# Moving the slice-weight products behind the row tiles of a graph-attention block loop on one Trainium2 core

## The reference, cut to what matters

```
x = x + gnn(layernorm(x), edges)
x = x + ffn(layernorm(x))

gnn:  support = x @ W;  r = sigmoid(support @ a2);  gated = r * support
      out  = segment_sum(edge_weight * gated[dst], src) / segment_sum(edge_weight * r[dst], src)
      l    = softplus(out @ a1);  out = elu(max(out, 0) + l * min(out, 0))

ffn:  w     = softmax((x @ W_x + b_x) @ W_slice ...) over 64 slices, for each of 8 heads
      token = sum over all nodes of w * (x @ W_fx), divided by the sum of w
      attention among the 64 tokens of a head, then out = w @ tokens @ W_out + b_out
```

## Time and profile before

| what | value |
|---|---|
| device time, median of 3 runs | 1400.97 us (1393.98 to 1402.22) |
| profiled execution: span from the first to the last instruction | 1658.8 us |
| PE busy | 1228.8 us, 74% of the span |
| DVE busy | 1036.5 us, 62% |
| POOL busy | 898.6 us, 54% |
| ACT busy | 540.6 us, 33% |
| mean granted TensorE clock | 0.851 |

### The profile page before, as it was taken

How to read it: one execution, slowest core, us unless ns; L and a number is a source line. 1 busy time by engine, 2 the same in 40 slices (tenths; PEclk the granted TensorE clock), 3 DMA queues, 4 the chain that set the end, 5 groups by cost and what they waited for, 6 DMA issues and landing times.

```text
span 1658.8 us, 22400 instructions
## 1 busy us (share of the span) xinstructions
PE 1228.8 (74%) x6239; PEld 983.0 (59%) x6239; DVE 1036.5 (62%) x2696; ACT 540.6 (33%) x1992; POOL 898.6 (54%) x895
## 2 busy tenths in 40 slices
PE   3797565767667668778688778786688676777998
PEld 2686464656666667756355555554456454555787
DVE  8778585766776766563466666565666656666422
ACT  2354243442442432401133323332333322333232
POOL 0476755555565455575666666666666666663000
PEclk9799778888889788877798989887888788888999
DMA  7123333634344344453534334533343433332122
GB/s 236 43 70 54 92 98 108 106 107 118 98 119 110 91 115 109 112 115 89 107 106 106 106 101 114 101 107 104 104 112 99 104 99 108 102 101 59 37 76 72
DMA packets 163423, 166.44 MB, mean 100 GB/s; under 512 B 84678, under 2 KB 135898, under 8 KB 163309
## 3 DMA queue, kind: packets, MB, share of 16 engines
q0 software_dynamic: 39712, 108.02, 24.9%
q1 hardware_dynamic: 102428, 37.71, 9.6%
q10 hardware_dynamic: 21168, 19.35, 3.9%
HBM read 136.86 MB, written 28.14 MB: 99 GB/s over the span
## 4 chain that ended last, share of the span: by engine, by line
issue 41%; PE 22%; DVE 14%; another core or an unknown queue 14%; ACT 5%; DMA 1%; POOL 1%; SPq 1%; POOLq 0%; DVEq 0%; ACTq 0%
PE bank L1733 22%; DVE S L1302 2%; DVE neg L1340 1%; ACT big L1675 1%; DVE ag L1313 1%; DVE lg L1328 1%; DVE hm L1323 1%; POOL rows L844 1%; ACT S L1656 1%; DMA rows<-gated_rows_dram,ring_i 1%; ACT xT L1662 1%; SPq L626 1%; ACT pos L1634 1%; DVE neg L1345 0%
## 5 line engine op out<-in xcount | busy, mean ns | idle before, releaser
L844 POOL DMA_INDIRECT rows<-gated_rows_dram,ring_i x516 | 512.4, 993 | 282.4 <-issue 144.7
L1733 PE MATMUL bank<-rows,S 128*128 128x257 f32 (+1 forms) x2254 | 580.2, 398 | 47.4 <-issue 21.6
L1733 PEld LDWEIGHTS bank<-rows,S 128*128 128x128 f32 x2254 | 439.6, 202 | 157.7 <-issue 75.0
L751 POOL DMA_INDIRECT rows<-gated_rows_dram,lg x294 | 287.5, 978 | 240.3 <-PE bank L1733 114.5
L1733 PE MATMUL bank<-big 128*104 128x128 f32 (+3 forms) x1824 | 250.7, 305 | 85.2 <-ACT big L1516 44.3
L1733 PEld LDWEIGHTS bank<-big 128*104 128x104 f32 (+2 forms) x1824 | 246.2, 210 | 92.2 <-issue 89.5
L1733 PE MATMUL bank<-Wxs,xT 128*128 128x512 f32 x196 | 148.0, 898 | 103.8 <-ACT xT L1662 103.8
L1516 ACT ACTIVATE big<-big 128x52 f32<-128x52 bf16 x768 | 180.0, 325 | 13.6 <-ACT ovr L1571 12.2
L1302 DVE TENSOR_SCALAR S<-iota,lof,srec 128x128 f32<-128x128 f32 x588 | 165.2, 357 | 3.2 <-remote 3.1
L1733 PEld LDWEIGHTS bank<-Wxs,xT 128*128 128x128 f32 x196 | 47.3, 266 | 158.2 <-ACT xT L1662 112.7
L1313 DVE TENSOR_TENSOR ag<-bank,ovr 128x257 f32<-128x257 f32 x49 | 20.9, 427 | 191.6 <-PE bank L1733 97.5
(11 more groups left out here) (261 smaller groups left out, 1486.9 us busy)
## 6 DMA issues: line engine op xcount, KB each, us to landing
overflow_sums_dram<-ovr ACTq DMA_DIRECT2D x98, 128.5 KB
rows<-gated_rows_dram,ring_i POOLq DMA_INDIRECT x516
gated_rows_dram<-rows SPq DMA_DIRECT2D x49, 128.5 KB, 2.5
ovr<-overflow_sums_dram SPq DMA_DIRECT2D x49, 128.5 KB
rows<-gated_rows_dram SPq DMA_DIRECT2D x49, 128.5 KB
out_dram<-S SPq DMA_DIRECT2D x48, 128.0 KB, 1.7
rows<-gated_rows_dram,lg POOLq DMA_INDIRECT x294
res<-in_x_dram SPq DMA_DIRECT2D x1, 4352.0 KB
```

Of the source, the lines that this page charges most:

```text
L751: pool.indirect_dma_start(rows[:, turn(n), :], None, gtab[:, :], bass.IndirectOffsetOnAxis(ap=ring1[:, n:n + 1], axis=0)).then_inc(s_row[t ...
L844: pool.indirect_dma_start(rows[:, slot(b, u), :], None, gtab[:, :], bass.IndirectOffsetOnAxis(ap=ring_i[:, b // CH % 2, n:n + 1], axis=0)) ...
L1733: return nc.tensor.matmul(o, l, r, start=start, stop=stop, skip_group_check=True)
```

## The change

Four edits:

- In the PE loop `logits(b-1)` moves from between tiles 6 and 7 to between tiles 10 and 11, in front of the block's last row tile; `own` stays behind tile 7.
- `scored` uses the mark of tile 11 in place of that of tile 7.
- In ACT's `main`, `crossed(b-1)` moves from in front of `expo` to behind the normalisation (`xn`), in front of `keep`.
- `xn` has four buffers (`XB`) in place of three. To make room, `ring_r` and `lof` (edge places, read as per-partition scalars) lie in the columns of `Ws2`, a weight tile that only stage 1 uses.

```diff
+XB = 4
...
-        ring_r = sb("ring_r", [P, 2, U])
+        ring_r = Ws2[:, 96:96 + 2 * U].rearrange("p (k t) -> p k t", k=2)
...
-        lof = sb("lof", [P, 2, CH * TQ])
+        lof = Ws2[:, 0:2 * CH * TQ].rearrange("p (k t) -> p k t", k=2)
...
-        xn = sb("xn", [P, 3, F])
+        xn = sb("xn", [P, XB, F])
...
         def scored(b):
-            return after(b, 2, MARKS[1], s_lm)
+            return after(b, 2, MARKS[3], s_lm)
...
                 if b < LAST:
                     own(b + 1)
-                if b:
-                    crossed(b - 1)
                 if b >= 2:
                     expo(b - 2)
...
                 act.wait_ge(s_rs, b + 1)
-                if b >= 3:
-                    act.wait_ge(*summed(b - 3))
-                a.activation(xn[:, b % 3, :], res[:, b, :], ACT.Identity,
+                if b >= XB:
+                    act.wait_ge(*summed(b - XB))
+                a.activation(xn[:, b % XB, :], res[:, b, :], ACT.Identity,
                              bias=col(NM), scale=col(RS)).then_inc(s_xn, 1)
+                if b:
+                    crossed(b - 1)
                 if b >= 3:
                     keep(b - 3)
...
                     cross(b - 1)
-                segment(b + 1, 3, 7)
+                segment(b + 1, 3, 8)
+                own(b + 1)
+                segment(b + 1, 8, TQ - 1)
                 if b:
                     logits(b - 1)
-                segment(b + 1, 7, 8)
-                own(b + 1)
-                segment(b + 1, 8, TQ)
+                segment(b + 1, TQ - 1, TQ)
```

More of the change, by code:

```diff
@@ L1952, in cross @@
                 for c in range(2):
-                    t = nc.tensor.transpose(bank[6][:, c * P:(c + 1) * P], xn[:, b % 3, c * P:(c + 1) * P], ident[:, :])
+                    t = nc.tensor.transpose(bank[6][:, c * P:(c + 1) * P], xn[:, b % XB, c * P:(c + 1) * P], ident[:, :])
                 if b + 2 > LAST:
@@ L1979, in sums @@
                 for c in range(lo, hi):
-                    m = mm(bank[2 + c // 2][:, (c % 2) * F:(c % 2 + 1) * F], w[:, c * P:(c + 1) * P], xn[:, b % 3, :], False, False)
+                    m = mm(bank[2 + c // 2][:, (c % 2) * F:(c % 2 + 1) * F], w[:, c * P:(c + 1) * P], xn[:, b % XB, :], False, False)
                 if hi == NP2 and b + 4 > LAST:
```

## The result

| kernel | median, us | runs | lowest to highest |
|---|---|---|---|
| before | 1399.16 | 20 | 1393.96 to 1405.24 |
| after | 1404.74 | 20 | 1397.74 to 1413.88 |

The ratio is 1.0036, with a 95% interval of 1.0021 to 1.0051: 3 to 7 us slower, 5.6 by the medians. The forecast was 1406 us (+5), "same" by the 1% bound. The median, the sign and the size agree with it. Whether they do so for the reasons given is what the rest of this text asks.

A forecast was written before the change was run, and what follows sets the result against it. The prediction took POOL's indirect gathers, 1.258 us from start to start, to bound the kernel. Loop 0 and end +5 us on the unprofiled median of 1401 gave 1406 us, range 1380 to 1440.

The forecast's parts named there:

- The gathers pace the loop: Block loop: POOL's gathers, 1.258 us apart, set the time; 1406 us, 57% together with the end's cost being hidden.
- The 13.25 of the prediction: Block loop: a block costs its 10.53 gathers at 1.258 us each, 13.25 us.
- the 19 that were left over: Block loop, shared with the sorting stage: at most about 19 us of POOL waiting left in an unprofiled run.
- Late marks belong to one execution: Block loop: PE's marks, up to some 10 us late, belong mostly to the profiled execution; rival (real everywhere): 1382 us, 18%.
- a sum (1362 us of work in a median of 1401): Whole kernel: if POOL never waited it would take 1362 us, leaving about 39 us of waiting unprofiled.
- The stage change: Between sorting stage and block loop: some 20 us of POOL's unprofiled waiting lie here.
- Two of the signs named for the profile after: Block loop: ScalarE's copy no longer held for "remote" over 100 us; DVE's wait for `guess` far below 77 us.
- The new round of 11.2 us, hidden: PE's loop through copy and products: 11.2 us a block at full clock, 13.2 at half, hidden under the gathers' 13.25.
- The end, +3.5 to +6.6, taken as 5: After the loop's last gather: nothing covers the moved products and copy, +3.5 to +6.6 us, taken as 5.
- The first part: Loop end: products of block 46 fall between the last gathered tile and the last `take`, +1.82 to +3.35 us.
- The second part: Loop end: block 47's copy moves behind the last normalisation, delaying products and last transposes by 1.7 to 3.2 us.
- The fourth buffer at nothing: `xn` in the loop: the trace has no wait of `xn` for PE, so the freed wait is worth nothing.

The follow-up runs named there:

- second profile: The kernel before, unchanged, profiled once more: one time of 1393.78 us.
- the change with its end as before: Changed kernel, but products in PE's last loop iteration and the copy in ScalarE's last two blocks stand where they stood before: 1399.61 us, ratio 1.0008.
- tile 10 in front: Kernel before, with PE running tiles 9 and 10 of block 0 before the second group of own-row sums: 1393.91 us, ratio 0.9961.
- The two edits that give back one half or both: Kernel before with only PE's order and `scored` changed, ratio 1.0003; changed kernel with products and copy at the loop's end placed as before, 1.0008.

## Why the prediction was right

**The gathers pace the loop: right, and shown.** Their spacing is 1.258 us in the median step of every undisturbed profile of both kernels, and blocks take 13.41 us in the mean before (second profile) and after. The 13.25 of the prediction lacked the little that POOL still waits in the loop: behind the first 16 gathers 9.8 us before and 8.6 after, by the sum of steps over 1.257 us. Both are inside the 19 that were left over. Taking three gathers out of ten makes the loop 10.6 us a block.

**Late marks belong to one execution: right.** It was an inference from a sum (1362 us of work in a median of 1401); a second profile confirmed it. One term of that sum carried the disturbance: the 146 us from the last gather to the end were 1391.9 - 1252.4 = 139.5 in the second profile, so about 6 us more of waiting were left than the 39 of the prediction. The stage change was taken as 20 us of it, from the first profile. By the same measure (from the last gather of the sorting stage to the twelfth of the loop, less 12 steps) it is 17.7 us before (second profile) and 23.2 after, POOL's hold of 7.70 or 12.39 in it, so that term was right too. The sorting stage, which the prediction did not look into, has 19 more in both (its steps over 1.257 us, the longer writes of sorted edges with them). With the loop's 9 or 10 that is about 28, which the 19 and the 6 above and the 4 that the sum had for those writes hold. Two of the signs named for the profile after, the copy no longer held for "remote" and DVE's short wait for `guess`, say nothing for the change: the second profile of the kernel before shows the same.

**The new round of 11.2 us, hidden: right, shown from both sides.** It is in the timeline (11.26), it appears as the pace with seven gathers, and with ten it costs nothing that shows: the change with its end as before stands at 1.0008. The half clock, at which the round would have come to 13.2, was no exception: in 13 of the 45 blocks from 640 to 1245 us the products took over 3 us, where the full clock gives 1.98 (in 6 of 45 before; granted clock 0.95 and 0.97). The blocks took 13.41 us in the mean all the same: 13.2 still lies under the gathers' share. The sum lacked the blocks with decoded lists, whose copy comes at 9.1 us and not 8.4, and whose round without cover is 11.9 to 13.5; with ten gathers they are covered too, as POOL runs on through them.

**The end, +3.5 to +6.6, taken as 5: right, +4.6.** The first part was taken from 1.82 to 3.35 and came at 1.77, the full clock; the second from 1.7 to 3.2 and came at 2.87, near the half clock's value, as the 3.78 us of the last products show. That the sum lies so near the middle is partly luck, one part at the low end and the other near the high. These are single profiles: the first part depends on how far PE is behind the gathers when they end. The gap from the last gather to the last `take`, 5.13 and 6.90 us above, was 7.91 with three buffers and 7.75 in the kernel that has both tile 10 in front and the end as before.

The second part is partly the clock's. From the last `take` to the end it was 137.0 to 138.1 us in the five profiles with the copy moved there, and 134.4 to 134.5 in six of the eight without. In the other two, the kernel before with seven gathers and with tile 10 in front, it was 136.0 and 136.2, though their ends are unchanged. In these two, as in the five, the granted clock was 0.83 in the 20 us behind the last `take`; in the six it was 0.91 or 1.00. So some 1.7 of the 2.87 us go with the lower clock, which came with the moved copy each time, and twice without it. The end as a whole stays apart: from the last gather to the end of the span, where the gathers pace the loop, it was 139.4 to 142.2 us in five profiles with the old end and 143.7 to 146.0 in three with the new. The two edits that give back one half or both are what ties the parts to their causes.

**The fourth buffer at nothing: right.** `xn` waited for PE for 3.2 us in two blocks even with four buffers, and removing the buffer left the time where it was.

**What stays open.** The medians differ by 5.6 us, the ends by 4.6; the rest is inside the interval. The runs of the changed kernel have a lower granted clock than those of the kernel before (0.933 in the mean of 20 against 0.941 in that of 23), and within its 20 runs the slowest (1413.88 us) has the lowest, 0.924, and the fastest (1397.74) the highest, 0.943. In the loop this lower clock costs nothing that shows, since with the end as before it is 0.935 and the time is back; whether it adds to the end is not shown. The loop's profiles scatter by as much as the whole effect (the hold of 7.7 or 12.4 us alone), so no single span could have shown it. And what disturbed the first profile is not known.

## What to carry to other kernels

Before reading waits out of a profile, hold its span against the times of the runs; where they differ by far, add up the work of the pacing engine by its steps from start to start and see how much waiting the real time has room for. A step that lengthened an engine's round by a microsecond cost nothing that shows while another engine paced the loop, but at the loop's end nothing covers it any more, and there the price was paid once. Two moves that look independent can lean on each other: the later copy was harmless only together with the later products, and by itself it cost 87 us.

## What the hardware showed that was not expected

- An indirect gather's price hardly depends on its rows: 1.258 us from start to start for 128 rows of 1028 bytes, 1.212 for 64. To shorten such a loop, issue fewer gathers; half the rows gave under 4%.
- One profiled execution of an unchanged kernel can be 258 us longer than its runs (1658.8 against 1401), with PE's marks up to some 10 us behind its recorded matmuls, and the next one 1391.9. The page says so by its span and by its granted clock (0.851 against 0.947); the waits look like waits of the kernel.
- The same 36 matmuls took 4.68 or 7.76 us at the same place in two profiles, at a granted clock of 0.86 or 0.50, and POOL's hold behind them went from 7.70 to 12.39. Part of the spread of the runs (1394 to 1405 us) may come from there; that is not shown, since a hold is known for the profiled runs alone.
